# Transposes split around the A product, wave 1's loads ahead of the parameters, VectorE's early work reordered, and filter taps copied by ScalarE

## The reference

```python
def pair(p, Wa, ba, Wb, bb, Wg, bg, Wo, bo):
    a = p @ Wa + ba
    b = p @ Wb + bb
    g = sigmoid(p @ Wg + bg)
    ab = einsum('bijk,bikl->bijl', a, b)
    return g * ab @ Wo + bo

x = x + pair(_gn(x), ...)        # _gn: mean and variance over 2 channels, 64 rows, 64 columns
x = x + lax.conv_general_dilated(_gn(x), filt, window_strides=(2, 2), padding=((1, 2), (1, 2)),
        lhs_dilation=(2, 2), feature_group_count=64, ...)   # four taps of each 4x4 filter matter
```

## Time and profile before

| | |
|---|---|
| median of 3 runs | 63.88 us |
| lowest, highest | 63.22, 64.78 us |
| the profiled execution's own time | 63.02 us |
| its span, first to last instruction | 61.1 us |
| mean granted TensorE clock, share of full speed | 0.978 |
| TensorE matmuls busy | 47.3 us (77%) |
| VectorE busy | 41.8 us (68%) |
| GpSimd busy | 37.5 us (61%) |
| ScalarE busy | 29.1 us (48%) |
| share of the last chain on TensorE, VectorE, ScalarE, issue, GpSimd | 30%, 17%, 12%, 11%, 10% |

### The profile page before, as it was taken

The page is one execution under the profiler, slowest core; times in us unless marked ns, Lnnn a source line. Parts: engine busy times, 40 slices in busy tenths (PEclk is TensorE's granted clock), DMA queues, the critical chain, the costliest instruction groups (busy, mean ns, idle before and its releaser), DMA issues.

```text
span 61.1 us, 2455 instructions
## 1 busy us (share of the span) xinstructions
PE 47.3 (77%) x1038; PEld 35.8 (59%) x1038; DVE 41.8 (68%) x112; ACT 29.1 (48%) x54; POOL 37.5 (61%) x51
## 2 busy tenths in 40 slices
PE   3997989877897988979979976988789895691000
PEld 3995959534865965848956835965468753330000
DVE  1076199989835675983598984588889964999700
ACT  5400003424294144657068999258891707991000
POOL 1000409449999999980572946983973996599500
PEclk9999999999999999999999999999999999999965
DMA  0899990000000000000000004040004004000494
GB/s 0 241 341 355 398 354 5 0 11 0 0 11 0 0 0 16 0 0 11 0 0 11 0 0 172 11 157 26 0 5 172 4 25 153 0 5 0 172 350 165
DMA packets 2603, 4.84 MB, mean 79 GB/s; under 512 B 288, under 2 KB 416, under 8 KB 2592
## 3 DMA queue, kind: packets, MB, share of 16 engines
q1 hardware_dynamic: 2592, 4.69, 21.3%
HBM read 2.59 MB, written 2.10 MB: 77 GB/s over the span
## 4 chain that ended last, share of the span: by engine, by line
PE 30%; DVE 17%; ACT 12%; issue 11%; POOL 10%; DVEq 2%; ACTq 0%; POOLq 0%
POOL y L250 7%; PE ps_ab L617 6%; PE ps_ot L657 5%; ACT rt L299 5%; ACT gate L312 4%; PE ps_ag L605 4%; PE ps_ot L584 4%; DVE y L449 4%; DVE part L391 3%; DVE ps_ab L464 3%; PE ps_ag L629 2%; PE ps_s L572 2%; DVEq L55 2%; PE ps_s L567 2%; PE ps_ab L641 1%
## 5 line engine op out<-in xcount | busy, mean ns | idle before, releaser
L250 POOL TENSOR_TENSOR y<-y,prod 128x512 f32<-128x512 f32 x11 | 14.0, 1274 | 5.4 <-DVE y L449 5.0
L215 POOL TENSOR_TENSOR rstd<-veps,half 128x2 f32<-128x2 f32 (+1 forms) x7 | 5.3, 759 | 11.2 <-DVE veps L419 11.2
L244 POOL TENSOR_TENSOR xb<-xs,par 128x512 f32<-128x512 f32 x8 | 8.6, 1099 | 1.6 <-issue 1.6
L559 PE MATMUL ps_ab<-zeros 128*128 128x128 f32 x54 | 8.5, 316 | 1.0 <-DVE zeros L467 1.0
L312 ACT ACTIVATE gate<-ps_ag,par 128x512 f32<-128x512 f32 x8 | 5.5, 688 | 7.5 <-PE ps_ag L629 7.5
L338 ACT ACTIVATE prod<-x,coef 128x512 f32<-128x512 f32 x11 | 7.5, 712 | 2.0 <-POOL coef L227 2.0
L559 PEld LDWEIGHTS ps_ab<-zeros 128*128 128x128 f32 x54 | 7.8, 226 | 1.0 <-DVE zeros L467 1.0
L305 ACT ACTIVATE at<-ps_ag,par 128x512 f32<-128x512 f32 x8 | 5.5, 686 | 5.6 <-PE ps_ag L605 5.6
L299 ACT ACTIVATE rt<-ps_ot 128x512 f32<-128x512 f32 x7 | 3.9, 595 | 8.7 <-PE ps_ot L584 8.7
L391 DVE BATCH_NORM_STATS2 part<-xs 128x6 f32<-128x512 f32 x8 | 5.4, 682 | 2.5 <-DMA xs<-x 2.4
L605 PE MATMUL ps_ag<-rt,par 64*64 64x256 f32 x64 | 5.3, 396 | 2.2 <-ACT gate L312 2.2
(11 more groups left out here) (59 smaller groups left out, 71.0 us busy)
## 6 DMA issues: line engine op xcount, KB each, us to landing
xs<-x SPq DMA_DIRECT2D x8, 256.0 KB, 4.3
out<-y SPq DMA_DIRECT2D x8, 256.0 KB, 2.1
par<-params SPq DMA_DIRECT2D x1, 353.0 KB, 3.5
par<-params SPq DMA_DIRECT2D x1, 128.0 KB, 2.9
```

Source lines behind the costliest of these rows:

```text
L244: nc.gpsimd.tensor_tensor(xb[:, w, b, :, :], xs[:, w, b, :, :], bo.broadcast_to([128, ROWS, D]), ALU.add).then_inc(xb_ready, 1)
L250: return nc.gpsimd.tensor_tensor(y[:, w, b, :, :], y[:, w, b, :, :], prod[:, n % 2, k, :, :], ALU.add)
L559: nc.tensor.matmul(bank[:, 0:128], zeros[:], zeros[:], start=True, stop=True)
```

## The change

Five things are different.

1. TensorE: in units 3 and 5 T(w + 1, 0) now stands ahead of A(g), and only T(w + 1, 1) stays between B(g) and G(g). The half n waits for x1_out of its own bank alone. ScalarE copies out T(w + 1, 0) ahead of `a_out(g)` and T(w + 1, 1) after the filter product. Unit 1 keeps its order.
2. SyncE: the two loads of wave 1 are issued ahead of the parameters.
3. VectorE's early order: x_part(1, 0) ahead of the normalisation of wave 0, x_part(1, 1) ahead of the copy of T(0, 1), which is cut into two halves so that A(0) waits for the first half alone. b_out(0) stands ahead of variance(1), and two of the x_parts of waves 2 and 3 move from unit 0 to unit 1.
4. The two copies of the taps into terms go from VectorE (L490) to ScalarE, after the first `transposed_out`; the reduction to tsum moves to unit 1, with a semaphore of its own that ScalarE waits for in `halo_out`.
5. GpSimd: the four diag instructions move from after add_bo(1) to after add_bo(3).

```diff
@@ sync
             sp.dma_start(par[:, 0:MASKS], params[:, 0:MASKS]).then_inc(masks_in, 16)
+            for b in range(2):
+                load(1, b)
             sp.dma_start(par[:, MASKS:], params[:, MASKS:]).then_inc(params_in, 16)
-            for w in range(1, WAVES):
+            for w in range(2, WAVES):
@@ gpsimd
             add_bo(1)
-            pool.wait_ge(taps_ready, 1)
-            for k in range(4):
-                last = nc.gpsimd.tensor_scalar(diag[:, k, :], ident, taps[:, LAST, k:k + 1], 0.0, ALU.mult, ALU.add)
-            last.then_inc(diag_ready, 1)
             add_bo(2)
...
             add_bo(3)
+            pool.wait_ge(taps_ready, 1)
+            for k in range(4):
+                last = nc.gpsimd.tensor_scalar(diag[:, k, :], ident, taps[:, LAST, k:k + 1], 0.0, ALU.mult, ALU.add)
+            last.then_inc(diag_ready, 1)
@@ scalar
             act.wait_ge(params_in, 16)
+            for b in range(2):
+                last = nc.scalar.activation(terms[:, :, b, 0:4].rearrange("p w (a b) -> p w a b", b=2),
+                                            ftap[:, :, 1:4:2, 1:4:2], ACT.Copy)
+            last.then_inc(taps_ready, 1)
...
                 else:
+                    if 1 <= w < LAST:
+                        transposed_out(w + 1, 0)
+                    a_out(g)
                     if w >= 2:
                         filter_product(w - 2, 0, 1)
-                    if w + 1 < WAVES:
+                    if w == 0:
                         transposed_out(w + 1, 0)
+                    if w < LAST:
                         transposed_out(w + 1, 1)
@@ vector
             variance(0)
+            x_part(1, 0)
             dve.wait_ge(rstd_done, 1)
...
-            x_part(1, 0)
+            link(x_part(1, 1))
             dve.wait_ge(t_done, 2)
-            nc.vector.tensor_copy(rows_of(rt[:, 0, :], 1), by_image(ps_ot[:, 1, :])).then_inc(rt0_dve, 1)
-            link(x_part(1, 1))
+            for n in range(2):
+                nc.vector.tensor_copy(rows_of(rt[:, 0, :], 1)[:, 8 * n:8 * n + 8],
+                                      by_image(ps_ot[:, 1, :])[:, 8 * n:8 * n + 8]).then_inc(rt0_dve, 1)
             aggregate(1)
             x_part(2, 0)
-            deviation(1)
...
                 if g == 0:
+                    deviation(1)
+                    b_out(0)
                     variance(1)
-                    b_out(0)
-                    x_part(2, 1)
-                    x_part(3, 0)
                     z_out(0)
                 elif g == 1:
+                    x_part(2, 1)
+                    b_out(1)
+                    x_part(3, 0)
                     link(x_part(3, 1))
-                    b_out(1)
                     aggregate(2)
...
@@ tensor
-                        pe.wait_ge(x1_ready, 2 * w - 2)
+                        pe.wait_ge(x1_ready, 2 * w - 3 + n)
...
-                if g == 0:
-                    pe.wait_ge(rt0_dve, 1)
+                if g < 2:
+                    pe.wait_ge(rt0_dve, g + 1)
...
+                else:
+                    transposes(w + 1, 0)
+                    product_a(g)
+                    product_b(g)
+                    transposes(w + 1, 1)
+                product_g(g)
+                product_ab(g)
```

More of the change, by code:

```diff
@@ L132, in preact_pair_mix_blur @@
         taps_ready, diag_ready, nt_ready = sem("taps_ready"), sem("diag_ready"), sem("nt_ready")
+        tsum_ready = sem("tsum_ready")
         pad_ready, halo_done, halo_ready = sem("pad_ready"), sem("halo_done"), sem("halo_ready")
@@ L318, in halo_out @@
                 act.wait_ge(minus_ready, X1JOB + w + 1)
+                act.wait_ge(tsum_ready, 1)
                 nc.scalar.activation(x1[:, w, :, :, D],
@@ L342, in _ @@
             act.wait_ge(params_in, 16)
+            for b in range(2):
+                last = nc.scalar.activation(terms[:, :, b, 0:4].rearrange("p w (a b) -> p w a b", b=2),
+                                            ftap[:, :, 1:4:2, 1:4:2], ACT.Copy)
+            last.then_inc(taps_ready, 1)
             for g in range(UNITS):
                 w, n = divmod(g, 2)
-                a_out(g)
                 if n == 0:
+                    a_out(g)
                     if w >= 2:
@@ L496, in _ @@
                 if g == 0:
+                    deviation(1)
+                    b_out(0)
                     variance(1)
-                    b_out(0)
-                    x_part(2, 1)
-                    x_part(3, 0)
                     z_out(0)
                 elif g == 1:
+                    x_part(2, 1)
+                    b_out(1)
+                    x_part(3, 0)
                     link(x_part(3, 1))
-                    b_out(1)
                     aggregate(2)
+                    dve.wait_ge(params_in, 16)
+                    nc.vector.tensor_reduce(tsum[:], ftap[:, :, 1:4:2, 1:4:2], mybir.AxisListType.XY,
+                                            ALU.add).then_inc(tsum_ready, 1)
                     z_out(1)
@@ L691, in _ @@
                 w, n = divmod(g, 2)
-                product_a(g)
                 if g == 0:
+                    product_a(g)
                     stat_product(1, 0)
@@ L696, in _ @@
                     stat_product(1, 1)
-                    product_g(g)
-                    product_ab(g)
                 elif n == 0:
                     job = 2 if g == 2 else X1JOB + w - 2
+                    product_a(g)
                     stat_product(job, 0)
@@ L706, in _ @@
                     product_o(w - 1)
-                    product_g(g)
-                    product_ab(g)
-                else:
+                elif g == 1 or w == LAST:
+                    product_a(g)
                     product_b(g)
-                    if w + 1 < WAVES:
+                    if g == 1:
                         transposes(w + 1, 0)
                         transposes(w + 1, 1)
-                    product_g(g)
-                    product_ab(g)
+                else:
+                    transposes(w + 1, 0)
+                    product_a(g)
+                    product_b(g)
+                    transposes(w + 1, 1)
+                product_g(g)
+                product_ab(g)
             idle_products(2, ps_ot[:, 0, :])
```

## The result

The changed kernel's median over 12 runs is 63.31 us (62.12 to 65.61), the kernel before now has 63.26 (62.85 to 64.78, 12 runs). The ratio of the fast runs alone, those within 1.5% of the fastest of their kernel, which are only 4 of the changed kernel's 12, is **0.9886, with a 95% interval of 0.9838 to 0.9934**, or 0.7 us less (0.4 to 1.0). By the 2% that the prediction used, this is "same", as forecast. The size was given as 0.4% and this ratio puts it at 1.1%, with the sign that was forecast; the two medians show no gain. How much of the 0.7 us is the change is therefore read from the stages further down.

What follows compares the result with a forecast made beforehand. No engine is full and the clock stays at its upper level, so order alone bounds the kernel. The terms 0.65 - 0.66 + 0.24 gain 0.23 us, giving 63.6 us against the median of 63.88, range 62.3 to 64.5.

Steps and rivals of the forecast that it cites:

- Part 1: Up to A(0): wave 1's moved load is hidden; the halved copy gains 0.09 us, so A(0) at 10.51.
- Part 2: Up to A(2): earlier mv, bsb(0) and zt(0), T(1) held by gn; A(2) at 18.06, gain 0.65 us.
- Part 3: A(2) to A(4): T(2, 0) waits 1.0 us for gn and holds A(3); loss 0.66 us.
- Part 4: A(4) to A(6): in unit 5 ScalarE's 0.25 us wait ahead of at(5) goes; gain 0.24 us.
- The rest: The taps' copies on ScalarE and the later diag on GpSimd fall in spare time and cost nothing.
- Sum: Whole kernel: 0.65 - 0.66 + 0.24 = 0.23 us gain, 63.6 against the median of 63.88.
- Rival A: Unit 3: gn(2) comes before AB(2) ends, so the wait does not bite; 62.6 us, chance 0.12.
- Rival B: Unit 3's wait bites and VectorE or wave 1's load eats the lead-in's gain; +0.4 us, 64.3, chance 0.18.
- rival C: Unit 3: the 1.0 us wait lowers TensorE's clock to 1.2 GHz; +3.5 us, 67.2, chance 0.03.

Runs made afterwards that it cites:

- e1: The changed kernel again, no edit, for a second trace and more runs; ratio 0.9916 to the kernel before, median 63.19 us.
- e8: The changed kernel with unit 3's split undone and the two statistics of waves 2 and 3 back in unit 0; ratio 0.9805, median 62.22 us.
- e9: The same kernel as e8 once more, for its time over more runs; ratio 0.984 to the kernel before, median 62.21 us.
- e3: The changed kernel with the split of the transposes undone in unit 3 alone, and ScalarE's copies with it; ratio 0.9864, median 62.84 us.
- e11: The changed kernel with GpSimd's four diag instructions put back between add_bo(1) and add_bo(2); ratio 1.006, median 63.69 us.
- e4: The kernel before with the split of the transposes in unit 5 alone; ratio 0.9967, median 63.29 us.
- e5: The kernel before with the new order of the loads alone, wave 1's slabs ahead of the parameters; ratio 0.9976, median 63.68 us.
- e10: The kernel of e9 with four products of zeros ahead of T(0, 0) in place of seven; ratio 0.9884, median 62.5 us.
- e6: The kernel of e3 with the masks issued between wave 0's two slabs; median 63.9 us against 63.6 for the kernel before.
- e12: The kernel of e9 with the masks issued first of all, ahead of both slabs of wave 0; ratio 0.9873, median 62.83 us.

## Why the prediction was right, point by point

**The prediction's own test.** It called itself wrong if A(6) did not come at 35.5 within 0.5. In the profile after, A(6) comes at 36.70, so by that test it fails there; in e1, the same kernel, it comes at 35.82 and passes. All of the 1.2 us lies ahead of A(0), which was 1.6 late (12.14 against 10.51), and the three stages behind it were 0.07, 0.19 and 0.19 shorter than forecast. What held is the path from A(0) on, and what did not is the lead-in.

**Part 1.** "Between 0 and 0.1 us" for A(0) was the weak step. The copy's halves did what was said (A(0) starts where the idle products end, 0.98 behind their start in e1, e8 and e9). But the start of the lead-in is not the 10.60 of one trace. It scattered from 10.48 to 12.91 over all traces, and two things that I had not priced lie in it: the landing of the masks, and when TensorE's speed doubles. I had asked where the moved slabs and the parameters land, and not what they do to the transfer ahead of them.

**Part 2.** Forecast 0.65 with the 0.09 of A(0), so 0.56 from A(0) to A(2); measured 0.62. B(0) was forecast 0.90 behind A(0), and is. T(1) was to be held by gn, and is. The clearing of VectorE ahead of zt(0), which I had counted among the reasons, was not needed beside the others (e8).

**Part 3.** The mechanism was right: a wait of 1.0 us for gn ahead of T(2, 0), A(3) forecast 5.50 behind A(2) and measured at 5.53, the whole shown by e3 and e11. The rule of program order on TensorE that I had cited from the Trainium skill, "TensorE: Matmul & The Clock Gate", the step-by-step section of Part 2, agrees with the four traces that had the wait: in none did A(3) start ahead of T(2, 0). The term was mis-sized: A(2) to A(4) costs 0.47 more than before, not 0.66. I took A(3) to T(2, 1) as 1.30, the old distance, but 0.2 of that was B(3) waiting for zt(2), and a late A(3) finds zt(2) done. It measured 1.06 (26.21 - 25.15). The row of before that I had not read, weight loads of B(3):

```profile
23.77 0.56 PEld L617 LDWEIGHTS ps_ab<-par,rt 64*64 64x64 f32 x32 [0.47 <-DVE zt L435]
```

A(3) to B(3) is 0.68 there and 0.48 in the profile after. A stall that makes everything late also uses up the other waits behind it.

**Part 4.** Forecast 0.24, measured 0.43 (e4). The 0.25 us hole ahead of at(5) is counted from the end of the product before it, but consecutive activations overlap: prod at 33.00 lasts 0.71 and the copy behind it starts at 33.62, 0.09 before its end. So closing that hole gives 0.34. The other 0.07 to 0.09 is a wait that no row named: the copies of T(3) in the kernel before started 0.69 behind T(3), at 33.86, when ScalarE could have started them at 33.79. In the kernel before:

```profile
31.62 0.71 ACT L338 ACTIVATE prod<-x,coef 128x512 f32<-128x512 f32 x1
...
33.17 1.09 PE L584 MATMUL ps_ot<-par,gn 128*128 128x128 f32 x8
33.17 0.71 ACT L338 ACTIVATE prod<-x,coef 128x512 f32<-128x512 f32 x1
...
33.86 1.09 ACT L299 ACTIVATE rt<-ps_ot 128x512 f32<-128x512 f32 x2
```

The Trainium skill, "ScalarE: Activation LUTs", section "What ACT_TABLE_LOAD costs", gives about 93 ns for that overlap of back-to-back ACTIVATEs; the trace agrees, and an estimate from it at the outset would have given 0.34 for the hole.

**The rest.** The taps on ScalarE cost nothing, as said: its wait ahead of at(0) is still 1.12 us long behind them. Diag on GpSimd was priced right in the kernel before (0.1), and wrongly as a part of this change: with A(2) 0.6 us nearer to A(0), its old place would have cost 0.7 (e11).

**Sum.** 0.62 - 0.47 + 0.43 = 0.58 us from the stages A(0) to A(6), against 0.23 forecast for the whole (0.14 for these stages), and against 0.72 (0.4 to 1.0) and 0.53 (0.2 to 0.9, e1) by the ratios. The difference comes from parts 3 and 4, the two terms that were mis-sized, each by 0.19 the same way. That the 63.6 lies within 0.3 us of the measured median of 63.31 is in part luck: it stood on a median of 63.88 from three runs, which is 63.26 over twelve, and 0.23 less than that would have been 63.03.

**Rivals.** Rival A is out, since the wait bit. Rival B, slower because the lead-in gives nothing, is out in its mechanism for VectorE, since A(0) to A(2) gave 0.62. But its other clause, that the load of wave 1 eats what was gained, is not: its sign was an A(2) at 18.7, and in e1 A(2) comes at 18.74. There, and in the profile after, the later A(0) took all that the stages gave, and the median of the 12 runs, 0.05 above that of the kernel before, fits it; in e8 and e9 the runs gained what the stages gave, with the same loads. The clock of rival C did not fall behind the wait of 1.0 to 1.7 us ahead of T(2, 0) in any of four traces that had it. The reason given against it was too strong, though. The wait of 1.10 us near the end left the products behind it at full speed in the trace of before (2.84 us for 6 records), but in five of the 14 traces, the profile after among them, they took 4.54, and the clock line falls to 5 tenths there:

```profile
53.71 4.54 PE L687 MATMUL ps_ag<-x,diag 128*128 128x512 f32 x6 [1.10 <-ACT x L323]
```

It cost little: two of the five, e5 and e11, have a tail of 25.4 and 25.5 us, as the kernel before has.

**What stays open.** Over the eight traces in which wave 1's slabs follow the masks these landed 3.0 to 4.4 us after their issue, over three with the parameters behind them 2.8 to 3.0. That is a trend with an exception (3.0 in e11), and e5's time did not show it. Why the masks are late in some executions, and whether the changed kernel's A(0) is later on average than that of the kernel before, was not settled: each trace is one execution, and those of e3, e9 and e10 were the slowest of their six.

## What to carry to other kernels

Work moved into a hole ahead of a held instruction is free only if its own input is there by then: look up when that input is ready, not only how long the hole is, and decide unit by unit (the same edit gained 0.43 us in unit 5 and lost 0.47 in unit 3). Compare the starts of the same instruction between two traces, stage by stage: the stages repeated to 0.02 us where whole executions scattered by 1 to 2 us. And a part of a change can be worth nothing by itself and still carry another part, as the loads did for the early statistics and diag's move for the wait on gn.

## What the runs showed of the hardware that was not expected

- **The start's speed.** In every trace the first records of zeros start 0.21 us apart, and later ones 0.11 apart. The speed doubled between 3.9 and 7.2 us from the span's start in eleven traces and at 9.9 to 10.3 in three (the changed kernel, e3, e10). The clock line shows 9 tenths from the start on in all three; the records show half speed and the line does not. Fourteen records of zeros lasted 1.81 us in ten traces and 2.91 to 3.27 in the changed kernel, e3 and e6; in these A(0) came 6.3 to 6.4 us behind the first product of statistics, in the others with the changed lead-in and no late slab 5.3 to 5.8. Why the speed doubled late in some executions stays open: TensorE waited 0.38 us ahead of that product in e10 and 0.37 in e3, but also 0.37 in the kernel before, where it doubled at 3.9.
- **A fall after a wait.** In e6 the speed had doubled by 4.3, TensorE then waited 1.57 us for mv, and from 7.5 to 10.9 the records are 0.21 apart again. This fall the clock line does show, as 5 tenths. With the five falls behind the wait of 1.10 near the end, it shows waits of 1.1 to 1.6 us that were followed by half speed in some executions; the waits of 1.0 to 1.7 us ahead of T(2, 0) were in none of four.
- **Small transfers are not cheap neighbours.** With 128 KB of masks ahead of it in the queue, the second 256 KB slab's statistics began at 5.47 (e6) and 4.97 (e12), in one trace each; with both slabs first, VectorE had done both by 4.5 to 5.0.
